# Causal mask of 9 of 12 self tiles by ScalarE, three score buffers in the self pass, and two more cross tiles bounded by VectorE

## The chip, the cores and the metric

One NeuronCore of a Trainium2 chip runs the whole kernel. The metric is device time in microseconds (us), the median of a few executions. The engines are PE (TensorE), ACT (ScalarE), DVE (VectorE), POOL (GpSimd) and SP (SyncE, which here only issues DMAs).

## What is computed

One pre-norm decoder layer on x of shape [32, 256, 256] (batch, sequence, width) in fp32, with 16 heads of 16:

```
x = x + selfattn(layernorm(x))          # latent q and kv projections, rotary, 4 kv heads, causal
x = x + crossattn(layernorm(x), ctx)    # q from x, k and v from ctx [32, 256, 256], one mask [256, 256]
x = x + ffn(layernorm(x))               # 256 -> 1024 -> 256, relu, values rounded to an 8-bit float
```

Softmax is exact: the row maximum of each head is subtracted before the exponential, and scores have fp32 accuracy, reached by cutting q and k into three bf16 parts whose six products are stacked along the contraction dimension (96 rows).

## The kernel before, in words

The batch is cut into 16 groups of two sequences (512 tokens, four blocks of 128). `body(i, prev, nxt)` is the software-pipelined loop body: it holds the attention of group i, the end of the cross attention and the feed-forward part of group i-1, and the projections for the self attention of group i+1. Each engine has its own copy of `body`, its instructions in a fixed, hand-written order; semaphores join them. `body(0)` and `body(15)` stand outside the hardware loop, and after `body(15)` comes an END part. One pass of the loop takes about 102.4 us.

Each attention has two passes. In the first, PE computes score tiles of [128 queries, 1024], DVE takes the row maxima of each (`row_max`), and the negated maxima are cut into three bf16 parts (`cut_first`, `cut_second` on ACT, `cut_rest`, `cut_third` on POOL), transposed by PE (`turn_max`), copied by ACT (`maxima`) and put by a small DMA of SP (`put_neg`) below the rows of Q. There is one such chain for each of the two sequences. In the second pass PE computes the transposed scores with the maxima already subtracted (`self_shifted`, `cross_shifted`), ACT takes the exponential into P (`exponentials`), masked places are set to zero or bounded, and PE multiplies with V three tiles later (`times_v`).

On PE the body runs these stages in order:

- E2, second pass of cross attention of group i-1: `attend(1, ...)`, 16 tiles. At t = 1 it holds the first half of the cross keys' projection of group i (`key2(st, 0)`), at t = 3 the transposes for the second sequence's maxima; tiles 8 to 15 wait for that sequence's `put_neg(1, 1)`. At its end stand self tiles 0 and 1 of group i.
- S1, first pass of self attention of group i: 12 tiles (8 with 256 keys of 4 heads, 4 with 128 keys of 8 heads), with the other projections of ctx between them (`tokens "v2"`, `key2(st, 1)`), then `tokens "out2"`.
- E1, second pass of self attention: 12 tiles and 3 steps.
- a middle part with the normalisations' transposes and the projections of group i+1.
- S2, first pass of cross attention of group i: 16 tiles, with the feed-forward products of group i-1 between them.

Score tiles of S1 alternate between two PSUM buffers, `score[0]` and `score[1]`; those of S2 use `o_pair` as a third. In S1 the causal mask of each tile is added by PE itself, with two matmuls of the identity and `causal_q` (lines 1346 and 1356). In S2, 14 of 16 tiles are handled otherwise: ACT writes the mask into the PSUM buffer ahead (`premask`, line 828), and PE's score matmuls accumulate on it. In E2, 12 of 16 tiles have their P bounded by DVE (`bound`, line 1053, an elementwise minimum with `cross_bound`), and tiles 3, 7, 11 and 15 get a mask from PE (line 1424).

SP issues in a fixed order, each DMA after its own wait. In the part around the border of two bodies it is: `put_part("q1", 0)` (three DMAs of 256 KB), `put_neg(1, 0)`, `put_part("k1", 0)`, `put_part("q1", 1)`, `put_part("k1", 1)`, and in the next body `put_neg(1, 1)`, `put_part("q1", 2)`, `put_part("k1", 2)`, the load of x.

Of the kernel before, what the change touches and what calls it, by code (L numbers as in the profile page):

```python
# [20 lines left out]
BATCH, SEQ, DM = 32, 256, 256  # L21
# [20 lines left out]
PROLOGUE = ["xnT1_0", "xnT1_1", "qa", "q0", "q1", "k", "v_0", "v_1", "maskT", "boundT", "bias"]  # L42


def body_users(prev, nxt):
# [8 lines left out]
    attention = (["k2_0"] + p("m2T_1") + ["v2_0", "k2_1", "m1T_0", "v2_1"] + p("out2_0", "out2_1")  # L54
# [71 lines left out]
def layer(nc, d):  # L126
# [9 lines left out]
    with ExitStack() as stack:  # L136
# [33 lines left out]
        causal_q = sb("causal_q", [128, 128], bf16)  # L170
# [68 lines left out]
        cross_bufs = [score[0], score[1], o_pair]  # L239
# [53 lines left out]
        TILE0 = {"S1": 0, "E1": N1, "E2": 2 * N1 + 2 * CROSS_USES[0]}  # L293
        TILES = 2 * N1 + 2 * CROSS_USES[0] + N2
# [8 lines left out]
        BOUNDED = (N1 - 2, 3 * UNITS)  # L303

        def bounded(a, t):


            u, s = t // TPU[a], t % TPU[a]
            if a == 0:
                return t - (t > 2) if t not in (2, N1 - 1) else None  # L310
            return 3 * u + s if s < 3 else None
# [6 lines left out]
        def cross_use(g, t):  # L318

            n = CROSS_BUF[t]  # L320
            return n, g * CROSS_USES[n] + CROSS_BUF[:t].count(n)

        def cross_tile(g, t):

            n, use = cross_use(g, t)
            return (n, use) if n == 2 else (n, g * (TILES // 2) + N1 + CROSS_BUF[:t].count(n))

        def cross_masked(g, t):

            n = CROSS_BUF[t]  # L330
            told = [u for u in range(N2) if u not in PE_MASKED and CROSS_BUF[u] == n]
            return n, g * len(told) + told.index(t)
# [20 lines left out]
        def _(sp):  # L353
# [80 lines left out]
            def body(i, prev, nxt):  # L434
# [23 lines left out]
                if nxt:  # L458
                    sp.wait_ge(small_full[st.bank("v2_1")], st.this("v2_1"))
                    sp.dma_start(ctxT[:, :, :], ctx_v[i + 1]).then_inc(ctx_loaded, 16)  # L460
                    put_part("q1", 0, i + 1)
                put_neg(st, 1, 0)
                if nxt:
                    put_part("k1", 0, i + 1)
# [16 lines left out]
        def _(pool):  # L481
# [14 lines left out]
            G.affine_select(out=causal_q[:, :], in_=causal_q[:, :], compare_op=ALU.is_ge, fill=-BIG,  # L496
# [124 lines left out]
            def body(i, prev, nxt):  # L621
# [3 lines left out]
                if nxt:  # L625
                    inverse_root(0, i + 1)
# [6 lines left out]
                cut_third(0, i, 1)  # L633
                for t in range(N1):
# [8 lines left out]
                if nxt:  # L643
                    rope_products("q1", cosq, sinq, q1s, i + 1)
                    rope_sum("q1", q1s, i + 1)
                    rope_products("k1", cosk, sink, k1s, i + 1)
                    rope_sum("k1", k1s, i + 1)
                    part("q1", 0, whole, part1, i + 1)
                cut_rest(1, i, 0)
                cut_third(1, i, 0)  # L650
                if nxt:
                    rest("q1", i + 1)
# [8 lines left out]
                if prev:  # L661
                    if nxt:
                        n, before = tile("S1", i + 1, 0)
# [15 lines left out]
        def _(act):  # L679
# [52 lines left out]
            def cut_first(a, g, b):  # L732

                last = N1 // GB * (b + 1) - 1
                for t in (last, last - 1) if a == 0 else last_cross_tiles(b):
                    n, before = tile("S1", g, t) if a == 0 else cross_tile(g, t)
# [24 lines left out]
            def exponentials(st, a, g, with_keys=False, last=False):  # L761
# [13 lines left out]
                for t in range(n):  # L775
# [7 lines left out]
                    if t == 1 and with_keys:  # L783
                        keys(st, 0)
# [37 lines left out]

            def premask(g, t):
# [4 lines left out]
                A.activation(cross_bufs[n][:, :, :].rearrange("p c (j k) -> p (c j) k", j=2),  # L828
# [59 lines left out]
            def body(i, prev, nxt):  # L888
                st = BODY(i)
                if prev:  # L890
                    cut_first(1, i - 1, 1)
                    exponentials(st, 1, i - 1, with_keys=True)
                else:
                    keys(st, 0)
# [946 lines left out]
```

## Time and profile before

| | |
|---|---|
| median of 3 executions | 1729.31 us (1727.02 to 1732.74) |
| profiled execution | 1726.77 us, its span 1725.1 us |
| mean granted TensorE clock | 0.982 of full |
| PE matmuls busy | 1617.5 us, 94% of the span |
| DVE, ACT, POOL busy | 67%, 65%, 44% |
| one pass of the loop | 102.4 us |

The span runs from the first to the last instruction of the profiled execution; its own time is 1.7 us more. A busy share is an average over all stages. In a timeline a row gives the start, the time to the end of the last instruction of the row, engine, line, what is written and read, how many instructions, and in brackets how long the engine sat idle before it and what released it.

### The profile page before, as it was taken

What the parts mean: (1) busy time and instruction counts of PE and PEld (TensorE: products, weight loads), DVE (VectorE), ACT (ScalarE), POOL (GpSimd) and SP (SyncE); (2) the same over time, 40 slices, a digit from 0 to 9 for tenths busy, and PEclk for the clock granted to TensorE, in tenths of its full rate; (3) what the DMA queues carried; (4) which work ended last, traced back from release to release, by engine and by line L of the source; (5) the groups of instructions that cost most, each with busy time, mean ns of one, the idle gap of its engine ahead of it and who ended that gap; (6) DMA issues with size and microseconds to landing.
All of it is one profiled execution on the core that took longest, in us unless ns stands there. A gap on an engine that the chain in (4) does not pass through costs nothing.

```text
span 1725.1 us, 33722 instructions
## 1 busy us (share of the span) xinstructions
PE 1617.5 (94%) x11950; PEld 973.6 (56%) x11950; DVE 1159.0 (67%) x1736; ACT 1116.1 (65%) x1733; POOL 753.5 (44%) x1010
## 2 busy tenths in 40 slices
PE   3879999999999999999999999999999999999988
PEld 2445556656555565655656555665655556565555
DVE  4557576685857758586676858668585775857573
ACT  4455675766668566665856567576666856666574
POOL 2252344644345553444545334464434555344410
PEclk7979999999999999999999999999999999999999
DMA  7473453754547374553845546375454737454420
GB/s 182 59 99 70 68 85 65 103 95 64 96 60 107 68 96 90 75 84 57 119 72 81 94 66 89 65 103 95 64 96 60 106 68 96 90 75 73 62 40 13
DMA packets 106238, 140.17 MB, mean 81 GB/s; under 512 B 12385, under 2 KB 74242, under 8 KB 105954
## 3 DMA queue, kind: packets, MB, share of 16 engines
q1 hardware_dynamic: 103090, 130.96, 51.0%
q0 software_dynamic: 2352, 8.26, 1.5%
q10 hardware_dynamic: 768, 0.57, 0.1%
q8 instruction: 18, 0.29, 0.1%
q14 instruction: 10, 0.08, 0.0%
HBM read 21.29 MB, written 8.39 MB: 17 GB/s over the span
## 4 chain that ended last, share of the span: by engine, by line
PE 75%; DMA 9%; ACT 6%; DVE 4%; issue 3%; POOL 2%; SPq 1%; DVEq 0%; ACTq 0%; POOLq 0%
PE o_pair L1457 14%; PE score L1418 8%; PE small L1543 7%; DMA Q<-negT 5%; PE small L1577 5%; PE o_pair L1288 5%; PE small L1288 4%; PE score L1395 3%; PE small L1304 3%; PE score L1341 3%; DVE negmax L1021 2%; PE score L1376 2%; PE small L1470 2%; DMA sums<-o_sb 2%; PE score L1400 2%
## 5 line engine op out<-in xcount | busy, mean ns | idle before, releaser
L1021 DVE TENSOR_REDUCE negmax<-score 128x4 f32<-128x1024 f32 (+1 forms) x384 | 456.9, 1216 | 73.4 <-PE score L1376 47.0
L780 ACT ACTIVATE P<-score 128x1024 f32<-128x1024 f32 x448 | 446.4, 1026 | 74.6 <-PE score L1418 26.4
L1053 DVE TENSOR_TENSOR P<-P,cross_bound 128x1024 f32<-128x1024 f32 x192 | 230.8, 1250 | 88.6 <-ACT P L780 88.5
L1457 PE MATMUL o_pair<-P,V 128*32 128x256 f32 (+1 forms) x4096 | 280.0, 362 | 2.6 <-DVE P L1053 2.4
L828 ACT ACTIVATE score<-cross_q 128x1024 f32<-128x1024 bf16 x192 | 196.3, 1023 | 46.4 <-DVE negmax L1021 42.9
L1418 PE MATMUL score<-Q,K 99*128 99x256 bf16 x1024 | 152.3, 276 | 25.9 <-DMA Q<-negT 24.8
L1457 PEld LDWEIGHTS o_pair<-P,V 128*32 128x32 f32 x4096 | 87.8, 108 | 134.6 <-issue 73.4
L1577 PE MATMUL small<-xnT,w 128*128 128x256 f32 x600 | 157.6, 381 | 0.0
L1418 PEld LDWEIGHTS score<-Q,K 99*128 99x128 bf16 x1024 | 83.7, 98 | 125.7 <-ACT P L780 61.7
L558 POOL TENSOR_TENSOR x<-x,ffn 128x1024 f32<-128x1024 f32 x15 | 32.8, 2189 | 268.9 <-DVE negmax L1021 268.9
L1376 PE MATMUL score<-K,Q 96*128 96x256 bf16 x768 | 121.0, 282 | 9.9 <-ACT score L828 5.4
L508 POOL TENSOR_TENSOR rstd<-vareps,minus_half 128x2 f32<-128x2 f32 x32 | 22.3, 698 | 236.1 <-DVE vareps L1002 236.1
L607 POOL TENSOR_SCALAR_AFFINE_SELECT P<-P 128x512 f32<-128x512 f32 (+1 forms) x160 | 121.7, 761 | 0.0
L1577 PEld LDWEIGHTS small<-xnT,w 128*128 128x128 f32 x600 | 103.4, 190 | 13.7 <-issue 0.2
L773 ACT ACTIVATE o_sb<-o_pair 128x512 f32<-128x512 f32 x128 | 75.9, 593 | 40.9 <-PE o_pair L1457 40.9
L1376 PEld LDWEIGHTS score<-K,Q 96*128 96x128 bf16 x768 | 74.3, 100 | 48.7 <-issue 13.6
L1041 DVE RECIPROCAL rsum<-small 128x16 f32<-128x16 f32 x63 | 16.2, 257 | 119.1 <-PE small L1470 119.1
L1341 PE MATMUL score<-K,Q 96*128 96x256 bf16 x512 | 79.1, 277 | 16.0 <-DVE negmax L1021 8.9
L1021 DVE TENSOR_REDUCE negmax<-o_pair 128x4 f32<-128x1024 f32 x64 | 78.4, 1225 | 18.0 <-PE o_pair L1381 18.0
L1288 PE MATMUL o_pair<-xnT,w 128*128 128x512 f32 x172 | 90.0, 618 | 0.0
L1341 PEld LDWEIGHTS score<-K,Q 96*128 96x128 bf16 x512 | 43.3, 98 | 68.4 <-DVE negmax L1021 36.3
L1086 DVE SCALAR_TENSOR_TENSOR q2f<-small,bq,q2p 128x256 f32<-128x256 f32 x64 | 28.0, 480 | 75.5 <-ACT q2p L813 75.5
(202 smaller groups left out, 3049.4 us busy)
## 6 DMA issues: line engine op xcount, KB each, us to landing
K<-k2p SPq DMA_DIRECT2D x96, 256.0 KB, 6.2
Q<-q2p SPq DMA_DIRECT2D x192, 128.0 KB, 5.2
Q<-q1p SPq DMA_DIRECT2D x90, 256.0 KB, 6.7
x_in<-in_x SPq DMA_DIRECT2D x16, 512.0 KB, 5.3
ctxT<-in_ctx SPq DMA_DIRECT2D x16, 512.0 KB, 7.1
k2f<-q1f SPq DMA_DIRECT2D x32, 256.0 KB, 6.3
inT<-o_sb SPq DMA_DIRECT2D x60, 128.0 KB
o<-inverse SPq DMA_DIRECT2D x60, 128.0 KB
```

What stands on the lines that cost most here:

```text
L607: G.affine_select(out=p, in_=p, compare_op=ALU.is_ge, fill=0.0, base=0, pattern=[[0, heads], [1, 128]], channel_multiplier=-1).then_inc(pr ...
L780: A.activation(P[:, t % 4, :], score[b][:, :, :], ACT.Exp, scale=SCALE).then_inc(score_free[b], 1)
L828: A.activation(cross_bufs[n][:, :, :].rearrange("p c (j k) -> p (c j) k", j=2), cross_q[:, t // 4 % 2, :].unsqueeze(1).broadcast_to([128, ...
L1021: V.tensor_reduce(negmax[:, k, h:h + 1024 // w], s.rearrange("p (h w) -> p h w", w=w), AX.X, ALU.max, negate=True).then_inc(score_free[b], 1)
L1053: V.tensor_tensor(p, p, cross_bound[:, t % 2, :].unsqueeze(1).broadcast_to([128, 4, SEQ]), ALU.min).then_inc(probs_masked[1], 1)
L1288: last = T.matmul(bank[0:rows, :], w[:, c, cols], src[:, c, :], start=c == 0, stop=c == NC - 1)
L1341: T.matmul(score[n][:, j // 2, SEQ * (j % 2):SEQ * (j % 2) + SEQ], Q1[0:KROWS, 4 * s + j, SEQ * b + 128:SEQ * b + 256], K1[0:KROWS, s, SEQ ...
L1376: last = T.matmul(cross_bufs[n][:, c, SEQ * j:SEQ * j + SEQ], Q2[0:KROWS, b, h, 128 * (k % 2):128 * (k % 2) + 128], K2[0:KROWS, h, SEQ * b ...
L1418: last = T.matmul(score[n][:, c, SEQ * j:SEQ * j + SEQ], K2[:, h, SEQ * b + 128 * kb:SEQ * b + 128 * kb + 128], Q2[:, b, h, :], start=j == ...
L1457: last = T.matmul(o_ps[ob][32 * j:32 * j + 32, SEQ * gg + q0:SEQ * gg + SEQ], v, p, start=s == 0, stop=end, tile_position=(0, 32 * j), ski ...
L1543: last = T.matmul(bank[:, DM * k:DM * k + DM], src[:, c, at:at + 128], w[:, c, :], start=c == 0, stop=c == NC - 1)
L1577: last = T.matmul(bank[:, half], w1[:, c, 128 * t:128 * t + 128], xnT3[:, c, half], start=p == 0, stop=c == NC - 1, skip_group_check=True)
```

## The change

- Self score tiles take three buffers in turn (`self_tile`: tile t in buffer t mod 3, `o_pair` third).
- Tiles 3 to 11 of S1 are no longer masked by PE: ACT writes the causal mask ahead (`self_premask`), nine times a body, in between its evictions of `v2` and `k2`. `causal_q` becomes 256 wide, with zeros in its first half. Tiles 0 to 2 keep their two matmuls.
- The first half of the cross keys' projection, `key2(st, 0)`, moves from E2 (t = 1) into S1, in two parts. The order there becomes v2, tile 2, v2, 3, k2, 4, k2, 5, k2, 6, k2, 7, v2, 8, v2, transposes, 9, 10, 11.
- E2: only tiles 3 and 15 are masked by PE; tiles 7 and 11 are bounded by DVE, 14 of 16 in all.
- DVE: `keys_rest` goes from the bounds to row maximum 5 of S1, and the statistics of the next x go behind row maximum 11.
- SP: `put_neg(1, 0)` goes ahead of `put_part("q1", 0)`. ACT and POOL cut the maxima of S2's first sequence somewhat earlier (`cut_first` before `premask` 10, `maxima` at tile 12 and not 13; on POOL the cuts before `rope_sum("k1")`).
- POOL: `inverse_root(0, i + 1)` goes behind the cuts of the second sequence.
- Prologue: 30 matmuls `warm0` without a use, before the `bias` product.

```diff
-        BOUNDED = (N1 - 2, 3 * UNITS)
+        MASK_ADDED = (3, N2 - 1)
+        BOUNDED = (N1 - 2, N2 - len(MASK_ADDED))
...
+        def self_tile(g, t):
+            n = t % 3
+            return n, g * (TILES // 2 if n < 2 else SELF_USES + CROSS_USES[2]) + t // 3
...
+                put_neg(st, 1, 0)
+                if nxt:
                     put_part("q1", 0, i + 1)
-                put_neg(st, 1, 0)
-                if nxt:
                     put_part("k1", 0, i + 1)
...
+            def self_premask(g, t):
+                n, before = self_tile(g, t)
+                act.wait_ge(score_free[n], before)
+                if t % 6 < 4:
+                    A.activation(bufs[n][:, :, :].rearrange("p c (j k) -> p (c j) k", j=2),
+                                 causal_q[:, :].unsqueeze(1).broadcast_to([128, 4, SEQ]),
+                                 ACT.Copy).then_inc(masked[n], 1)
...
-                    exponentials(st, 1, i - 1, with_keys=True)
-                else:
-                    keys(st, 0)
+                    exponentials(st, 1, i - 1)
+                self_premask(i, 3)
+                self_premask(i, 4)
                 values2(st, 0)
-                cut_first(0, i, 0)
-                cut_second(0, i, 0)
+                self_premask(i, 5)
+                keys(st, 0)
+                self_premask(i, 6)
                 keys(st, 1)
                 keys_full(st, 1)
+                self_premask(i, 7)
+                cut_first(0, i, 0)
+                self_premask(i, 8)
+                cut_second(0, i, 0)
+                self_premask(i, 9)
+                values2(st, 1)
+                self_premask(i, 10)
+                maxima(st, 0, 0)
+                self_premask(i, 11)
                 keys_second(st, i, 0)
-                maxima(st, 0, 0)
-                values2(st, 1)
                 keys_second(st, i, 1)
...
-                    if t == 1 and at_end == "scores":
-                        pe.wait_ge(ctx_loaded, 16 * (g + 2))
-                        key2(st, 0)
...
+            def warm(st, name, n):
+                bk = st.bank(name)
+                pe.wait_ge(small_free[bk], st.before(name))
+                for k in range(n):
+                    last = T.matmul(small[bk][:, :], identb[:, :], again(identb, 4), start=True, stop=True)
...
+            warm(PRO, "warm0", 30)
             bk = PRO.bank("bias")
...
-                self_scores(i, [2])
                 if not prev:
                     pe.wait_ge(loaded, 16 * LOADS)
-                    pe.wait_ge(ctx_loaded, 16 * (i + 1))
-                    key2(st, 0)
+                pe.wait_ge(ctx_loaded, 16 * (i + 1))
+                tokens(st, "v2", ctxT, wv2, 0, 0)
+                self_scores(i, [2])
+                tokens(st, "v2", ctxT, wv2, 0, 1)
                 self_scores(i, [3])
-                tokens(st, "v2", ctxT, wv2, 0, 0)
+                key2(st, 0, 0)
                 self_scores(i, [4])
-                tokens(st, "v2", ctxT, wv2, 0, 1)
+                key2(st, 0, 1)
                 self_scores(i, [5])
                 key2(st, 1, 0)
...
                 self_scores(i, [6])
                 key2(st, 1, 1)
                 self_scores(i, [7])
+                tokens(st, "v2", ctxT, wv2, 1, 0)
+                self_scores(i, [8])
+                tokens(st, "v2", ctxT, wv2, 1, 1)
                 turn_max(st, 0, i, 0)
-                self_scores(i, [8])
-                tokens(st, "v2", ctxT, wv2, 1, 0)
                 self_scores(i, [9])
-                tokens(st, "v2", ctxT, wv2, 1, 1)
```

## Rows read from the trace of the kernel before

**Rows 1.** The page, part 1: busy time of each engine.

```profile
PE 1617.5 (94%) x11950; PEld 973.6 (56%) x11950; DVE 1159.0 (67%) x1736; ACT 1116.1 (65%) x1733; POOL 753.5 (44%) x1010
```

**Rows 2.** Timeline of PE, stage E2 of one pass: start, us, instructions.

```profile
849.83 1.04 PE L1418 MATMUL score<-Q,K 99*128 99x256 bf16 x8 [1.62 <-DMA Q<-negT]
850.71 1.88 PE L1288 MATMUL small<-ctxT,wk 128*128 128x512 f32 x4
852.43 1.04 PE L1418 MATMUL score<-Q,K 99*128 99x256 bf16 x8
...
853.95 0.64 PE L1457 MATMUL o_pair<-P,V 128*32 128x256 f32 x8
...
855.63 0.61 PE L1418 MATMUL score<-Q,K 99*128 99x256 bf16 x4
...
857.85 0.61 PE L1418 MATMUL score<-Q,K 99*128 99x256 bf16 x4
...
859.40 0.61 PE L1418 MATMUL score<-Q,K 99*128 99x256 bf16 x4
```

**Rows 3.** The chain that ended last, in order of time: start, us, what.

```profile
843.59 6.11 DMA Q<-negT
...
873.68 2.19 DMA sums<-o_sb
```

**Rows 4.** Timeline of ACT, end of stage S2.

```profile
843.20 0.37 ACT L753 ACTIVATE negT<-small 48x256 bf16<-48x256 bf16 x1
...
848.80 0.23 ACT L739 ACTIVATE negparts<-negmax 128x32 bf16<-128x32 f32 x1
```

**Rows 5.** Timeline of DVE, three bounds of stage E2.

```profile
856.33 3.50 DVE L1053 TENSOR_TENSOR P<-P,cross_bound 128x1024 f32<-128x1024 f32 x3 [0.18 <-ACT P L780]
```

**Rows 6.** Timeline of SP: when DMAs are issued.

```profile
839.71 1.85 SPq L365 DMA_DIRECT2D Q<-q1p  x3
...
855.42 0.76 SPq L407 DMA_DIRECT2D Q<-negT  x1
```

**Rows 7.** One stretch: busy us of each engine, clock, DMA share, GB/s.

```profile
841.00:855.50 14.50, 12.35 (x97) 7.88 (x96) 9.89 (x10) 10.84 (x18) 10.38 (x13) 1.00 0.99 114
```

**Rows 8.** The page, part 5: a premask of ACT.

```profile
L828 ACT ACTIVATE score<-cross_q 128x1024 f32<-128x1024 bf16 x192 | 196.3, 1023 | 46.4 <-DVE negmax L1021 42.9
```

**Rows 9.** Timeline of PE, stage S1 of the same pass.

```profile
872.26 0.61 PE L1341 MATMUL score<-K,Q 96*128 96x256 bf16 x4
...
873.16 0.61 PE L1341 MATMUL score<-K,Q 96*128 96x256 bf16 x4
...
873.83 1.03 PE L1543 MATMUL small<-wv,ctxT 128*128 128x256 f32 x4
874.69 0.61 PE L1352 MATMUL score<-K,Q 96*128 96x128 bf16 x8
875.14 0.60 PE L1356 MATMUL score<-causal_q,identb 128*128 128x512 bf16 x2
...
886.22 1.89 PE L1543 MATMUL small<-wo,inT 128*128 128x256 f32 x8
```

**Rows 10.** Timeline of ACT, stage S1 of the same pass.

```profile
872.39 0.60 ACT L773 ACTIVATE o_sb<-o_pair 128x512 f32<-128x512 f32 x1 [2.10 <-PE o_pair L1457]
...
881.23 0.68 ACT L704 ACTIVATE k2f<-small,bk 128x512 f32<-128x512 f32 x1
881.80 0.63 ACT L722 ACTIVATE k2p<-k2f 128x512 bf16<-128x512 f32 x1
...
884.65 0.64 ACT L711 ACTIVATE V<-small 128x512 f32<-128x512 f32 x1 [1.97 <-PE small L1543]
885.17 0.61 ACT L722 ACTIVATE k2p<-k2f 128x512 bf16<-128x512 f32 x1
```

**Rows 11.** Timeline of PE: the bias product of the prologue, and the first E2.

```profile
32.92 2.07 PE L1629 MATMUL small<-wo,bv 128*128 128x256 f32 x4 [8.92 <-DVE cross_k L1152]
...
126.64 1.89 PE L1418 MATMUL score<-Q,K 99*128 99x256 bf16 x8 [3.26 <-DMA Q<-negT]
```

More of the change, by code:

```diff
@@ L39 @@
 SCALE = HD ** -0.5
-PROLOGUE = ["xnT1_0", "xnT1_1", "qa", "q0", "q1", "k", "v_0", "v_1", "maskT", "boundT", "bias"]
+PROLOGUE = ["xnT1_0", "xnT1_1", "qa", "q0", "q1", "k", "v_0", "v_1", "maskT", "boundT", "warm0", "bias"]
 def body_users(prev, nxt):
@@ L302, in layer @@
         EVICT_AFTER = (4, 6, 8, 11, 12)
-        BOUNDED = (N1 - 2, 3 * UNITS)
+        MASK_ADDED = (3, N2 - 1)
+        BOUNDED = (N1 - 2, N2 - len(MASK_ADDED))
         def bounded(a, t):
[L308 to L311, printed above, removed]
+            added = (2, N1 - 1) if a == 0 else MASK_ADDED
+            return t - sum(m < t for m in added) if t not in added else None
         def tile(phase, g, t):
@@ L316, in tile, with cross_tile, masked_told, masked_use @@
             return n % 2, g * (TILES // 2) + n // 2
-        def cross_use(g, t):
+        def self_tile(g, t):
+            n = t % 3
+            return n, g * (TILES // 2 if n < 2 else SELF_USES + CROSS_USES[2]) + t // 3
+        def cross_tile(g, t):
             n = CROSS_BUF[t]
[L321 to L332, printed above, removed]
+            use = CROSS_BUF[:t].count(n)
+            return (n, g * (SELF_USES + CROSS_USES[2]) + SELF_USES + use) if n == 2 else \
+                (n, g * (TILES // 2) + SELF_USES + N1 // 2 + use)
+        def masked_told(n):
+            return ([("S1", t) for t in range(SELF_PE_MASKED, N1) if t % 3 == n]
+                    + [("S2", t) for t in range(N2) if t not in PE_MASKED and CROSS_BUF[t] == n])
+        def masked_use(phase, g, t):
+            n = t % 3 if phase == "S1" else CROSS_BUF[t]
+            told = masked_told(n)
+            return n, g * len(told) + told.index((phase, t))
         def last_cross_tiles(b):
@@ L662, in body @@
                     if nxt:
-                        n, before = tile("S1", i + 1, 0)
+                        n, before = self_tile(i + 1, 0)
                         pool.wait_ge(score_free[n], before + 1)
@@ L734, in cut_first @@
                 last = N1 // GB * (b + 1) - 1
-                for t in (last, last - 1) if a == 0 else last_cross_tiles(b):
-                    n, before = tile("S1", g, t) if a == 0 else cross_tile(g, t)
+                for t in (last, last - 1, last - 2) if a == 0 else last_cross_tiles(b):
+                    n, before = self_tile(g, t) if a == 0 else cross_tile(g, t)
                     act.wait_ge(score_free[n], before + 1)
@@ L1011, in row_max @@
             def row_max(a, g, t):
-                b, before = tile("S1", g, t) if a == 0 else cross_tile(g, t)
+                b, before = self_tile(g, t) if a == 0 else cross_tile(g, t)
                 dve.wait_ge(score_full[b], before + 1)
-                s = (score[b] if a == 0 else cross_bufs[b])[:, :, :].rearrange("p c n -> p (c n)")
+                s = bufs[b][:, :, :].rearrange("p c n -> p (c n)")
                 if a == 0 and t % 6 >= 4:
@@ L1169, in cross_bounds @@
                         bound(g, t)
-                    if t == 3 and i is not None:
-                        keys_rest(st, i, 0)
                     if t in (9, 13) and i is None:
                         normalise(st, 1, t // 5 - 1, g)
-                    if t == 11 and nxt:
-                        dve.wait_ge(x_loaded, 16 * (i + 2))
-                        block_stats(0, x_in, range(3))
-                if nxt:
-                    norm_stats(0, x_in, i + 1, range(3, NBLK))
             def body(i, prev, nxt):
@@ L1335, in self_scores @@
                     b, s = t // 6, t % 6
-                    n, before = tile("S1", g, t)
-                    if positive(before):
+                    n, before = self_tile(g, t)
+                    by_pe = t < SELF_PE_MASKED
+                    if not by_pe:
+                        _, use = masked_use("S1", g, t)
+                        pe.wait_ge(masked[n], use + 1)
+                    elif n == 2:
+                        for ob in range(2):
+                            if positive(g * UNITS):
+                                pe.wait_ge(o_free[ob], g * UNITS)
+                    elif positive(before):
                         pe.wait_ge(score_free[n], before)
```

90 lines of the change are left out of this document (48 added, 42 removed).

## The prediction, made before the changed kernel ran

> **What bounds the kernel now.** I read the page first: PE's matmuls are busy 94% of the span, the other engines 67% or less [rows 1]. So a pass of the loop is PE's list of work plus PE's waits, and each edit is priced by what it does to PE's list and to PE's waits. Then I read PE's timeline over one pass (848 to 950 us), where two things stand out. First, E2 opens with a wait of 1.62 us for the DMA of the negated maxima [rows 2]. Second, the key projection that follows, 1.72 us from 850.71 to 852.43, fills time in which tile 2 could not have run for long anyway: it needs the buffer of exponential 0. The chain shows why the DMA is late: it takes 6.11 us, while a small transfer issued into an empty queue takes 2.19 [rows 3]. Behind that lies SP's timeline: three 256 KB transfers of q1 are issued at 839.71, ahead of it [rows 6], and from 841 to 855.5 the DMA engines are full, share 0.99 at 114 GB/s [rows 7].
>
> **Part 1, the start of E2: a gain of 1.9 us a pass.** `put_neg(1, 0)` no longer stands behind the q1 transfers, and ACT copies the maxima one premask (1.0 us) sooner, so it is issued at 843.59 - 1.0 = 842.6 and lands about 2.2 later, near 845 [rows 3, 4]. PE is free at 849.83 - 1.62 = 848.2 [rows 2]. Next late is ACT: its cut of the last maxima starts at 848.80 [rows 4], and with the overlap of 0.1 seen between ACT's instructions exponential 0 starts at 848.95 and ends at 849.97 (an exponential has the size of a premask, 1.02 us [rows 8]). Tile 2 then starts at 850.0, tile 3 after exponential 1 at 851.05, scores and mask take 0.44 each, the transposes 0.1, and the first product with V comes at 852.05 instead of 853.95 [rows 2]: 1.9. The key projection's removal is inside this; alone it would give about 0.5, because exponentials pace the start. If the cut by POOL comes late here, exponential 1 waits up to 1.0.
>
> **Part 2, two masks less in E2: 0.44 each.** Two tiles without a mask take 857.85 - 855.63 = 2.22, so 1.11 each, one with a mask 859.40 - 857.85 = 1.55 [rows 2]. Tiles 7 and 11 give 0.88. The cover is DVE's pitch: three bounds take 3.50 with the last about 1.25, so one each 1.13 [rows 5], against 1.11 of PE. Eleven in a row lag 0.2 behind, and the product comes three tiles later. I price it at nothing; should the pitch be 1.25, it costs 0.5.
>
> **Part 3, the second `put_neg`: a new wait of 2.1.** E2's tile 8 needs `put_neg(1, 1)`. Before, that was issued at 855.42, just as the queue ran empty, and tile 8 started at 859.40 without a wait [rows 2, 6]. Now it is issued 1.9 earlier, at 853.5, but the q1 and k1 transfers, issued from 839.71 before, start only behind the first `put_neg`, at 842.6 + 0.8 = 843.4, 3.7 later. They move the same bytes at full DMA share [rows 7], so they end near 855.2 + 3.7 = 858.9, and the small transfer, behind them in the same queue, lands near 859.2. Tile 8 is due at 859.40 - 1.9 - 0.44 = 857.06. PE waits 2.1. Nothing else of PE's list can pass it: the products with V stand behind. Bounds: 0, if the small transfer slips through in 2.2 us, and 3.9 more than a free one, the excess of the 6.11 over the 2.19 [rows 3], which gives up to 3.9. I take 2.1, nearer to what the first one shows. The Trainium skill says the same of the queue (DMA: Bandwidth & Descriptors, Queues, rings and completion order): on each DMA engine the descriptors of one issuing queue are consumed in ring order. By that rule the transfer cannot land before the backlog in front of it, and it speaks against moving q1 behind; the 6.11 us agrees.
> E2 in all: -1.9 - 0.88 + 2.1 = -0.7.
>
> **Part 4, S1: 2.7 us longer.** Before, from the last product of E2 to `out2` PE needs 886.22 - 872.26 = 13.96 [rows 9]. After, its own work is: v2 and k2 in eight pieces of 0.87 (874.69 - 873.83; a piece of k2 has as many columns), 6.9; tile 2 with mask 873.83 - 873.16 = 0.67; nine tiles of 0.44 to 0.45 (875.14 - 874.69), 4.0; transposes 0.1. That is 11.7. If ScalarE kept ahead, S1 would gain 2.3. But ACT's list interleaves premasks with evictions that must wait for PE, and PE's next tile waits for the premask behind the eviction. From the end of issue of a projection piece it is 0.19 until ACT starts (row 873.83 lasts 1.03 against 0.87 to the next, and a releaser adds 0.03), a key eviction takes 0.57 (881.80 - 881.23), an eviction of v2 0.52 (885.17 - 884.65) [rows 10], a premask 1.02, and 0.06 until PE starts.
> - Tile 6 waits for premask 6, behind `keys(0)`: 0.19 + 0.57 + 1.02 + 0.06 = 1.84, of which tile 5 and a k2 piece cover 1.31. Wait 0.5.
> - Tile 7 stands directly behind the last k2 piece, and its premask behind `keys(1)` and `keys_full(1)`: 0.19 + 2 x 0.57 + 1.02 + 0.06 = 2.4, nothing covers it. Wait 2.4.
> - Tile 10, behind `values2(1)`: 0.19 + 0.52 + 1.02 + 0.06 = 1.8, less transposes and tile 9, 0.56. Wait 1.2.
> - Tile 11: `maxima` (0.37 less overlap, about 0.3) and a premask (pitch 0.94) after tile 10, less 0.44. Wait 0.8.
> Sum 4.9 to 5.0, so S1 takes 16.7 instead of 13.96: +2.7. ACT starts on its premasks on time, right behind the eviction at 872.39. DVE is not the bound: twelve maxima of about 1.2, one reciprocal and `keys_rest` fit in between. The first chain of maxima lands before E1 (its DMA finds a free queue: 2.2 after `maxima`, which is 1.7 before E1 starts with `out2` in between), and the statistics now behind row maximum 11 end 0.4 before PE needs the bank that DVE's next instruction frees. So E1 follows without a new wait, and middle and S2 keep their length.
> The bounds of this term: 2.0, if the handovers between engines are each 0.1 to 0.2 shorter, and 3.5, if `out2`'s chain or E1's first DMA slips too.
>
> **Part 5, the ends.** The first E2 waits 3.26 for the DMA [rows 11]; at a low clock its projection is dear too. I take -3.5 there, and no wait at tile 8, as its tiles are slow. `warm0`: the bias product runs at half clock, 2.07 us for four matmuls that take 1.03 later [rows 9, 11]. Thirty matmuls of 512 columns at 0.43, falling to 0.22, take about 9 us from 32.92, in a gap that ends at about 41: bias, and behind it DVE's last rotary steps, are 2 to 3 us later, but group 0's S1 runs at full clock. +0.5, S1 of group 0 included. END has two masks less: -0.9.
>
> **The sum.** Fourteen passes of -0.7 + 2.7 = +2.0 give +28; the first pass -3.5 + 2.7 = -0.8; prologue +0.5; END -0.9. In all +27. The profiled execution took 1726.8 us, so 1754; the median of the three runs lies 2.5 above it, so 1757.
>
> **Rivals.**
> - The transfer is in time (0.18). The 24 KB slip through the backlog and tile 8 doesn't wait; then E2 gains 2.8, S1 loses 2.7, they nearly cancel, and with part 5 the time is about 1727. For it: rings are many, and the small rows may find a free one. Against: the 6.11 us.
> - Faster (0.14). The place is tiles 6, 7, 10 and 11 of S1. If their waits sum to 2.5 and not 5, S1 costs 0.2, a pass gains 0.5, and the time with part 5 is about 1719; with no waits at all 1681. It decides once the sum falls under 3.0. For it: PE removes 2.9 us of mask matmuls. Against: the order of ACT's list.
> - The clock falls (0.10). S1 becomes thin for PE (11.7 busy of 16.7). If the granted clock drops to its lower level of 1.2 GHz after tile 7's gap, the remaining 5.3 us of S1 and `out2` take twice as long, less the 2 us of waits that this hides: 3 more a pass, about 1800. Against: the wait of 1.62 before E2 left the clock at 1.00 in the stretch around it [rows 7]. The Trainium skill (TensorE: Matmul & The Clock Gate, HAM oscillation) describes loops that go back to half rate at each gap. No row here shows a gap of 2.4 us in a full pass.
> - Slower otherwise (0.08): POOL's cut is late in E2, or DVE's pitch is 1.25; 1765 to 1775.
> - My forecast has 0.50, with a range of its own of 1740 to 1774.
>
> **How the numbers follow.** 0.3% (5 us) is about what a measurement of this kernel can tell from no change. Slower: 0.50 + 0.10 + 0.08 and a little of the first rival, 0.72. Same: 0.12. Faster: 0.14 and a part of the first rival, as first pass and END gain, 0.16. The range goes from 1722, which leaves out the lower half of the faster case, to 1778, which leaves out the clock's.
>
> **What would show it.** In the profile after: no wait of line 1418 at E2's tile 0; a wait of 1 to 4 us for DMA Q<-negT at its tile 8; in S1 waits of PE for ACT's premask of about 0.5, 2.4, 1.2 and 0.8; S1 near 16.7; a pass near 104.4. ACT busy about 150 us more (16 x 9 x 1.02), PE about 55 us less. The prediction is wrong if ACT's premasks run ahead of PE in S1, if tile 8 doesn't wait, or if the clock falls.

## The result, and the profile of the changed kernel

The changed kernel takes 1874.24 us (median of 4 executions, 1872.49 to 1875.28) against 1728.94 for the kernel before (4 executions): 1.084 times the time, with an interval of 1.0823 to 1.0856. That is 145 us more, far above the forecast range. The page of the changed kernel, its part 1 and the clock line of part 2:

```profile
PE 1664.0 (89%) x11628; PEld 978.2 (52%) x11628; DVE 1201.6 (64%) x1768; ACT 1257.0 (67%) x1877; POOL 753.3 (40%) x1010
...
PEclk9979989999899998999999899998999999899999
```

PE has 322 matmuls fewer than in [rows 1], and yet it is busy 46.5 us longer. So the instructions are slower on average, and the mean granted clock fits that: 0.937, where it was 0.982. PE's waits, by what ended them (us in all, how many, the longest in us):

```profile
PE score L1446 <- DMA Q<-negT: 54.3, 14, 3.9
...
PE score L1372 <- ACT score L837: 43.0, 33, 2.3
```

The first comes once in a pass, at tile 8 of E2. The second comes twice, at tiles 6 and 7 of S1, hence the 33. Now one pass, stage E2, on PE's timeline (answers to [rows 2]):

```profile
913.04 1.04 PE L1619 MATMUL small<-w2q,hq 128*128 128x256 fp8e4 x8
913.91 1.22 PE L1446 MATMUL score<-Q,K 99*128 99x256 bf16 x8
915.93 0.61 PE L1446 MATMUL score<-Q,K 99*128 99x256 bf16 x4 [0.80 <-ACT P L791]
...
918.05 0.64 PE L1486 MATMUL o_pair<-P,V 128*32 128x256 f32 x8
...
927.08 1.03 PE L1446 MATMUL score<-Q,K 99*128 99x256 bf16 x4 [3.94 <-DMA Q<-negT]
928.04 1.08 PE L1486 MATMUL o_pair<-P,V 128*32 128x256 f32 x8
...
933.69 0.64 PE L1486 MATMUL o_pair<-P,V 128*32 128x256 f32 x8
```

Tile 0 has no wait any more, tile 8 waits 3.94. And look at the second number of each row: the same eight products take 0.64 at 918.05, 1.08 at 928.04 and 0.64 again at 933.69. The chain and SP's timeline show what tile 8 waits for (answers to [rows 3, 6]):

```profile
919.43 7.53 DMA Q<-negT
```

```profile
908.51 0.79 SPq L417 DMA_DIRECT2D Q<-negT  x1
909.42 1.88 SPq L375 DMA_DIRECT2D Q<-q1p  x3
...
914.55 1.25 SPq L373 DMA_DIRECT2D K<-k1p  x2
919.43 0.76 SPq L417 DMA_DIRECT2D Q<-negT  x1
920.45 0.57 SPq L375 DMA_DIRECT2D Q<-q1p  x1
921.07 0.58 SPq L373 DMA_DIRECT2D K<-k1p  x1
```

Stage S1 on PE's and on ACT's timeline (answers to [rows 9, 10]):

```profile
942.24 1.13 PE L1569 MATMUL small<-wv,ctxT 128*128 128x256 f32 x4
...
947.84 1.08 PE L1311 MATMUL small<-ctxT,wk 128*128 128x512 f32 x2
949.25 0.61 PE L1372 MATMUL score<-K,Q 96*128 96x256 bf16 x4 [0.34 <-ACT score L837]
949.70 1.02 PE L1311 MATMUL small<-ctxT,wk 128*128 128x512 f32 x2
953.00 0.61 PE L1372 MATMUL score<-K,Q 96*128 96x256 bf16 x4 [2.27 <-ACT score L837]
953.45 1.56 PE L1569 MATMUL small<-wv,ctxT 128*128 128x256 f32 x4
...
955.65 1.81 PE L1569 MATMUL small<-wv,ctxT 128*128 128x256 f32 x4
957.29 0.28 PE L1582 MATMUL small<-identb,negparts 128*128 128x128 bf16 x2
957.40 0.60 PE L1372 MATMUL score<-K,Q 96*128 96x256 bf16 x4
959.09 0.62 PE L1379 MATMUL score<-K,Q 96*128 96x128 bf16 x8 [1.08 <-ACT score L841]
960.29 0.76 PE L1379 MATMUL o_pair<-K,Q 96*128 96x128 bf16 x8 [0.58 <-ACT o_pair L841]
960.84 3.53 PE L1569 MATMUL small<-wo,inT 128*128 128x256 f32 x8
964.21 1.03 PE L1423 MATMUL score<-Q,K 99*128 99x512 bf16 x4
```

```profile
950.76 0.69 ACT L709 ACTIVATE k2p<-small,bk 128x512 bf16<-128x512 f32 x1 [1.56 <-PE small L1311]
951.35 0.68 ACT L715 ACTIVATE k2f<-small,bk 128x512 f32<-128x512 f32 x1
951.92 1.03 ACT L837 ACTIVATE score<-causal_q 128x1024 f32<-128x1024 bf16 x1
```

ACT's three rows are tile 7's wait: it stands idle until the last piece of k2 is there, evicts it twice, and only then writes the mask that PE has been waiting for since 950.7. The windows over these stages, with columns as in [rows 7]:

```profile
913.00:925.00 12.00, 8.91 (x86) 4.44 (x84) 9.37 (x8) 9.52 (x13) 3.81 (x6) 1.00 1.09 118
925.00:933.00 8.00, 5.92 (x36) 1.91 (x36) 2.49 (x3) 2.86 (x3) 0.00 (x0) 0.59 0.68 107
933.00:941.00 8.00, 8.00 (x85) 3.75 (x82) 6.93 (x6) 6.08 (x8) 0.00 (x0) 0.98 0.05 17
941.00:952.00 11.00, 9.39 (x65) 5.26 (x63) 9.31 (x9) 6.85 (x10) 2.99 (x2) 1.00 0.31 94
...
955.00:957.00 2.00, 2.00 (x9) 1.60 (x7) 1.11 (x1) 0.07 (x1) 2.00 (x3) 0.50 0.00 0
957.00:960.00 3.00, 1.63 (x16) 0.94 (x14) 1.59 (x3) 2.51 (x4) 3.00 (x4) 0.96 0.00 0
...
962.00:964.00 2.00, 2.00 (x7) 1.55 (x6) 1.96 (x10) 0.46 (x2) 0.49 (x2) 0.50 1.02 152
964.00:966.00 2.00, 2.00 (x11) 1.38 (x10) 1.65 (x5) 1.07 (x2) 1.03 (x1) 0.99 1.10 119
```

The clock falls to its lower level, 1.2 GHz, three times in a pass. Behind tile 8's wait it stays there for some 6 us, until 933. Behind tile 7's wait it is low from about 954 to 957. From there to 960 it is back at 2.4 GHz: tile 9's scores, at 957.40, take the 0.60 of full speed. Then, behind the waits of 1.08 and 0.58 at tiles 10 and 11, it falls once more and is back at 964, which makes `out2` slow. From 925 to 933, 5.92 us of PE's work hold 36 instructions; from 933 to 941, 8.00 us hold 85.

A pass takes 112.7 us, 10.3 more than before. By stage, from the starts of the rows above, of [rows 2, 9], and of the last feed-forward products before:

```profile
847.17 1.04 PE L1593 MATMUL small<-w2q,hq 128*128 128x256 fp8e4 x8
```

| stretch | before | after | change |
|---|---|---|---|
| last feed-forward product to first product with V | 6.78 | 5.01 | -1.8 |
| on to tile 8 of E2 | 5.45 | 9.03 | +3.6 |
| tile 8 to the end of E2 | 12.86 | 15.16 | +2.3 |
| S1 | 13.96 | 18.60 | +4.6 |
| out2 | 1.72 | 3.37 | +1.6 |

They add up to 10.3 or so, which leaves next to nothing for the other stages. Fourteen to fifteen such passes make the 145.

### The profile page after: what moved, and what is told of

It reads as the page before. It is cut to its first block, busy times and chain, and to the rows that moved or that the text cites. A ratio compares the mean times of both kernels' runs of the same rounds, so it can differ in the third digit from the quotient of the medians.

```text
span 1873.0 us, 33411 instructions
## 1 busy us (share of the span) xinstructions
PE 1664.0 (89%) x11628; PEld 978.2 (52%) x11628; DVE 1201.6 (64%) x1768; ACT 1257.0 (67%) x1877; POOL 753.3 (40%) x1010
## 4 chain that ended last, share of the span: by engine, by line
PE 74%; ACT 9%; DMA 7%; issue 5%; DVE 4%; POOL 1%; ACTq 0%; SPq 0%; DVEq 0%; POOLq 0%
PE o_pair L1486 11%; PE small L1569 10%; DMA Q<-negT 6%; PE score L1446 5%; PE small L1603 5%; PE o_pair L1311 4%; PE small L1311 4%; PE score L1404 3%; PE small L1619 3%; PE score L1423 3%; PE small L1327 3%; PE score L1372 2%; ACT P L791 2%; PE small L1499 2%; ACT score L837 2%
## 5 line engine op out<-in xcount | busy, mean ns | idle before, releaser
L1051 DVE TENSOR_REDUCE negmax<-score 128x4 f32<-128x1024 f32 x320 | 386.5, 1217 | 98.9 <-PE score L1404 43.3
L1083 DVE TENSOR_TENSOR P<-P,cross_bound 128x1024 f32<-128x1024 f32 x224 | 269.4, 1246 | 129.6 <-ACT P L791 129.5
L1486 PE MATMUL o_pair<-P,V 128*32 128x256 f32 (+1 forms) x4096 | 300.2, 384 | 3.4 <-DVE P L1083 3.2
L1446 PE MATMUL score<-Q,K 99*128 99x256 bf16 x1024 | 178.1, 303 | 74.9 <-DMA Q<-negT 54.3
L1051 DVE TENSOR_REDUCE negmax<-o_pair 128x4 f32<-128x1024 f32 (+1 forms) x128 | 156.3, 1221 | 56.3 <-PE o_pair L1384 22.4
L1404 PE MATMUL score<-K,Q 96*128 96x256 bf16 x768 | 119.7, 280 | 13.1 <-ACT score L850 8.8
L525 POOL TENSOR_TENSOR negrest<-negmax,negparts 128x32 f32<-128x32 f32 x64 | 16.5, 258 | 235.7 <-ACT negparts L750 235.7
L1404 PEld LDWEIGHTS score<-K,Q 96*128 96x128 bf16 x768 | 73.7, 99 | 51.4 <-ACT score L850 14.6
L1372 PE MATMUL score<-K,Q 96*128 96x256 bf16 x384 | 58.3, 274 | 43.0 <-ACT score L837 43.0
L1569 PE MATMUL small<-wv,ctxT 128*128 128x256 f32 x256 | 86.9, 474 | 0.0
```

Of the source, the lines that this page charges most:

```text
L1051: V.tensor_reduce(negmax[:, k, h:h + 1024 // w], s.rearrange("p (h w) -> p h w", w=w), AX.X, ALU.max, negate=True).then_inc(score_free[b], 1)
L1083: V.tensor_tensor(p, p, cross_bound[:, t % 2, :].unsqueeze(1).broadcast_to([128, 4, SEQ]), ALU.min).then_inc(probs_masked[1], 1)
L1372: last = T.matmul(bufs[n][:, j // 2, SEQ * (j % 2):SEQ * (j % 2) + SEQ], Q1[0:KROWS, 4 * s + j, SEQ * b + 128:SEQ * b + 256], K1[0:KROWS, ...
L1404: last = T.matmul(bufs[n][:, c, SEQ * j:SEQ * j + SEQ], Q2[0:KROWS, b, h, 128 * (k % 2):128 * (k % 2) + 128], K2[0:KROWS, h, SEQ * b:SEQ * ...
L1446: last = T.matmul(score[n][:, c, SEQ * j:SEQ * j + SEQ], K2[:, h, SEQ * b + 128 * kb:SEQ * b + 128 * kb + 128], Q2[:, b, h, :], start=j == ...
L1486: last = T.matmul(o_ps[ob][32 * j:32 * j + 32, SEQ * gg + q0:SEQ * gg + SEQ], v, p, start=s == 0, stop=end, tile_position=(0, 32 * j), ski ...
```

## The experiments

Two theories stand against each other: the waits alone (for the DMA and for the masks) cost the time, or the waits together with the clock that falls behind them.

**One edit taken back: the order of the first small transfer.** `e1_q1_first` is the changed kernel with

```diff
+                if nxt:
+                    put_part("q1", 0, i + 1)
                 put_neg(st, 1, 0)
                 if nxt:
-                    put_part("q1", 0, i + 1)
                     put_part("k1", 0, i + 1)
```

> The changed kernel, with the first q1 transfers issued ahead of put_neg(1, 0) again. Queue theory (the q1 and k1 transfers, moved behind the first small transfer, delay the second one): the wait of 3.94 us at tile 8 of E2 and the low clock after it (2.7 us) go, a wait of 0.5 to 1.0 at tile 0 comes back; a pass shrinks from 112.7 by about 6, to 106.6, and the time falls from 1874 to about 1789. S1 stays at 18.6 us. Rival (the low clock has another cause, such as the thin S1): the wait goes, but the clock stays low in E2; 1874 - 15 x 3.2 = 1826. Rival (the second small transfer is slow by itself): nothing changes.

Measured 1825.51 us, ratio 1.0558 (1.0533 to 1.0582), a pass 109.2. Tile 8 waits no more. Tile 0 does, for longer than before the change, and the low clock comes in the rows behind it, after two more waits of 0.76 and 0.42:

```profile
894.96 1.04 PE L1447 MATMUL score<-Q,K 99*128 99x256 bf16 x8 [2.42 <-DMA Q<-negT]
...
897.79 1.03 PE L1447 MATMUL score<-Q,K 99*128 99x256 bf16 x4 [0.42 <-ACT P L792]
```

So the edit alone is worth 49 us of the 145. The number is by chance that of the first rival, 1826, but the rival had the clock low in E2 without a wait; in the trace the rows behind tile 8 run at full speed. The expected time was too low for three reasons. Tile 0's wait is 2.42 and not 0.5 to 1: the q1 transfers are issued at 884.87, 6.6 us ahead of the last feed-forward product, where it was 7.5 before the change, and in both kernels the small transfer lands 10.0 us behind that issue. The low clock follows this wait too. And there is a new wait of 1.08 in E1, for the small DMA of S1's maxima. In the changed kernel, where `out2` is slow, it does not show; here `out2` runs at full clock in every pass, though the four waits of S1 are the same.

**One edit alone: the same order in the kernel before.** `e5_before_swap`:

```diff
                     sp.dma_start(ctxT[:, :, :], ctx_v[i + 1]).then_inc(ctx_loaded, 16)
+                put_neg(st, 1, 0)
+                if nxt:
                     put_part("q1", 0, i + 1)
-                put_neg(st, 1, 0)
-                if nxt:
                     put_part("k1", 0, i + 1)
```

> The kernel before, with one edit: put_neg(1, 0) ahead of put_part(q1, 0) on SP, as the change has it. Queue theory: the wait of 1.62 us at E2's tile 0 goes and one of 2 to 4 us comes at tile 8, with the low clock after it (2.7 us); a pass gets 3 to 5 us longer and the time is 1775 to 1805. Rival (the late second transfer comes from something else in the change, such as the shorter E2 start): E2 shrinks by 1.6 and the time is about 1705.

Measured 1795.23 us, ratio 1.0379 (1.0359 to 1.0400), as expected. Moving one small DMA ahead of three large ones costs 66 us, with the low clock behind the new wait as part of it:

```profile
889.83 0.61 PE L1418 MATMUL score<-Q,K 99*128 99x256 bf16 x4 [2.88 <-DMA Q<-negT]
```

**The order of ACT in S1.** `e2_premask_first` is the changed kernel with each premask ahead of the eviction that made it late:

```diff
                 self_premask(i, 5)
+                self_premask(i, 6)
                 keys(st, 0)
-                self_premask(i, 6)
+                self_premask(i, 7)
                 keys(st, 1)
                 keys_full(st, 1)
-                self_premask(i, 7)
...
+                self_premask(i, 10)
                 values2(st, 1)
-                self_premask(i, 10)
+                self_premask(i, 11)
                 maxima(st, 0, 0)
-                self_premask(i, 11)
```

> The changed kernel, with ACT's premasks of S1 ahead of the evictions that wait for PE (premask 6 before keys(0), 7 before keys(1), 8 behind keys_full, 10 before values2(1), 11 before maxima). Order theory (PE's waits in S1 come from ACT's order, and the low clock after them from the waits): the waits of 2.3 and 1.1 us go, the clock stays at 1.00 through S1, S1 takes 14 to 15 us and not 18.6, out2 1.7 and not 3.4; a pass shrinks by about 6 and the time is about 1784. Rival (ACT's total work of nine premasks is what makes S1 long, in whatever order): S1 stays near 18 us and the time above 1850. E2's wait of 3.9 stays in both.

Measured 1821.93 us, ratio 1.0537 (1.0511 to 1.0562). S1 takes 928.95 - 914.60 = 14.35 instead of 18.60, and `out2` behind it runs at full clock. But E2's wait of 3.84 stays, and E1 now waits twice:

```profile
928.49 0.62 PE L1379 MATMUL o_pair<-K,Q 96*128 96x128 bf16 x8 [0.84 <-ACT o_pair L841]
928.95 1.95 PE L1569 MATMUL small<-wo,inT 128*128 128x256 f32 x8
931.75 1.03 PE L1423 MATMUL score<-Q,K 99*128 99x512 bf16 x4 [0.86 <-DMA Q<-negT]
...
940.28 0.60 PE L1423 MATMUL score<-Q,K 99*128 99x512 bf16 x2 [1.30 <-DMA Q<-negT]
```

It is 38 us slower than expected, and these two, 2.2 us a pass, are most of that: the small DMAs of S1's maxima are late next.

**The clock by itself.** `e3_fill` leaves both waits as long as they are. It puts matmuls that nobody reads into them, 18 before tile 8 of E2 and 7 before tile 7 of S1:

```diff
+            def dummy(bk, before, n):
+                pe.wait_ge(small_free[bk], before)
+                for k in range(n):
+                    T.matmul(small[bk][:, :], identb[:, :], again(identb, 4), start=True, stop=True)
...
+                    if t == n // 2 and at_end == "scores":
+                        dummy(st.bank("v2_0"), st.before("v2_0"), 18)
...
                 key2(st, 1, 1)
+                dummy(st.bank("v2_1"), st.before("v2_1"), 7)
                 self_scores(i, [7])
```

> The changed kernel with matmuls without a use in its two largest waits: 18 of 512 columns into a free bank before E2's tile 8 waits for its DMA, 7 before S1's tile 7 (PE's order only; nothing else moves). It measures the clock's part alone. Clock theory: the waits stay for the other engines, but the granted clock stays at 1.00, and the 2.7 us of E2 and the 3.5 us of S1 and out2 that run at 1.2 GHz go: 1874 - 15 x 6.2 = about 1781. Rival (the waits alone cost what was lost, and the clock's part is small): above 1850.

Measured 1816.72 us, ratio 1.0507 (1.0482 to 1.0531), mean clock 0.981. PE's rows around tile 8:

```profile
898.10 4.06 PE L1293 MATMUL small<-identb 128*128 128x512 bf16 x18
902.02 0.61 PE L1452 MATMUL score<-Q,K 99*128 99x256 bf16 x4
```

Work without a use made the kernel 57 us faster: the wait is as long as before, but the tile behind it takes 0.61 and not 1.03. The waits of the changed kernel alone would thus have given 1817 or less, and the clock did the rest. Or less, because the clock is not held everywhere: behind S1's last two waits, 1.09 and 0.57, `out2`'s first eight matmuls take 1.95 in nine of fifteen passes, and 3.0 to 3.6 in the other six. The time lies 36 us above the expected one and 33 below the rival's. The wait of 1.08 in E1 comes out here in the passes where `out2` is fast, some 10 us in all, and the six slow rows make some 8; the other 18 were not looked into.

**Both edits of order.** `e4_both` is the first and the third experiment together.

> Both edits, q1 transfers first and premasks first. If the two causes add up: 1874 - 85 - 90 = about 1700, faster than before (1729) by 1.7%, as two masks less in E2 and S1 at 14.2 us remain. If the rest of the change has a cost of its own (DVE's longer list, the projection moved into S1), it ends at 1729 or above.

Measured 1786.26 us, ratio 1.0332 (1.0308 to 1.0357): 86 us too high. At tile 0 of E2 the wait is back, with a second one of 0.76 behind it and then rows at low clock; two more, 0.86 and 1.24, are in E1:

```profile
871.99 1.04 PE L1447 MATMUL score<-Q,K 99*128 99x256 bf16 x8 [2.45 <-DMA Q<-negT]
873.79 2.07 PE L1447 MATMUL score<-Q,K 99*128 99x256 bf16 x8 [0.76 <-ACT P L792]
```

Here my expectation fell, that the edits would take 85 and 90 us away. Alone they took 49 and 52, together 88. The kernel needs an order in which neither small transfer is issued while many large ones are still under way.

**Such an order.** In `e6_split`, again the changed kernel, the second part of q1 and k1 moves behind the second small transfer:

```diff
                     put_neg(st, 1, 1)
+                    put_part("q1", 1, i)
+                    put_part("k1", 1, i)
                     put_part("q1", 2, i)
...
                     put_part("k1", 0, i + 1)
-                    put_part("q1", 1, i + 1)
-                    put_part("k1", 1, i + 1)
```

> The changed kernel, with put_part(q1, 1) and put_part(k1, 1) moved behind put_neg(1, 1), so that each of the two small transfers has at most one batch of large ones in front of it. Queue theory: no wait at tile 0 of E2, none at tile 8, clock 1.00 in E2; S1 as in the changed kernel (18.4 to 18.6 us); a wait of about 1.1 at tile 6 of E1 appears as in e1. Against e1_q1_first (1825.5) a pass gains the difference of the waits at tile 0, 2.4 against none, so about 1800. Rival (the bytes of both batches delay whatever comes after): the wait moves to self tile 0, which needs all of q1 and k1, and the time stays at 1825 or above.

Measured 1778.00 us, ratio 1.0280 (1.0259 to 1.0300), a pass 105.9. No wait for a DMA is left in E2; S1's four waits are unchanged. The place of the four DMAs that moved had thus made 96 of the 145 us, the low clock in E2 included. The time is 22 us below the expected one: the wait that was expected in E1 comes only in the two passes of fifteen in which `out2` runs at full clock, and in the first.

**The clock in S1 by itself.** `e10_split_fill` is `e6_split` with `e3_fill`'s second edit, the 7 unused matmuls before tile 7 of S1.

> e6_split with seven matmuls without a use in the wait before S1's tile 7: the low clock's price in S1 and out2 alone. Clock theory: S1's other waits stay, the granted clock stays at 1.00 and about 3.5 us of S1 and out2 go, of which E1 may give back 1.1 in its wait at tile 6: 1778 - 15 x 2.5 = about 1741. Rival (the clock falls because S1 as a whole is thin, whatever is done in its one large gap): 1770 or more.

Measured 1753.34 us, ratio 1.0135 (1.0101 to 1.0170): 25 us less than `e6_split`, and nearer to the clock theory's 1741 than to its rival's 1770. S1 takes 794.78 - 777.95 = 16.83, where the forecast had 16.7. The row behind it still shows the low clock, as it does in six of fifteen passes:

```profile
777.95 1.13 PE L1575 MATMUL small<-wv,ctxT 128*128 128x256 f32 x4
...
794.78 3.61 PE L1575 MATMUL small<-wo,inT 128*128 128x256 f32 x8
```

**All of it in order.** `e7_best` has `e6_split`'s SP, `e2_premask_first`'s ACT, and

```diff
-                self_premask(i, 11)
                 maxima(st, 0, 0)
+                self_premask(i, 11)
...
                 put_neg(st, 0, 0)
-                put_part("k2", 0, i)
                 put_neg(st, 0, 1)
-                for n in range(1, 3):
+                for n in range(3):
```

> The split order of e6, the premasks ahead of the evictions as in e2, and for E1: maxima ahead of premask 11 on ACT, both small transfers of S1 ahead of all k2 transfers on SP. If every lost microsecond has been named (waits at tiles 0 and 8 of E2, S1's order, waits of 0.9 and 1.2 in E1, the clock after them): a pass takes 101.2 us, against 106.2 in e4_both, and the time is about 1712, faster than before by 1%. If the change's other parts cost something, 1729 or more. If the DMAs only move their delay, 1750 or more.

Measured 1702.34 us, ratio 0.9842 (0.9826 to 0.9859), clock 0.981, a pass 100.7: the first version that beats the kernel before, by 1.6%, and 10 us better than expected. S1 takes 771.36 - 756.78 = 14.58, with three small waits, the last of them

```profile
770.91 0.62 PE L1378 MATMUL o_pair<-K,Q 96*128 96x128 bf16 x8 [1.08 <-ACT o_pair L840]
```

**Two masks back on PE.** `e11_best_masks` is `e7_best` with `MASK_ADDED = (3, 7, 11, N2 - 1)`, as before the change.

> e7_best with E2's tiles 7 and 11 masked by PE again, as before the change. If each of them costs PE 0.44 and DVE has room for it: 16 x 0.88 = 14 us more than e7_best (1702), 1716. Rival (DVE's pitch or the exponentials bound E2 then, so PE's masks are hidden): 1702 to 1706.

Measured 1715.61 us, ratio 0.9922 (0.9895 to 0.9950): 13.3 us over 16 passes is 0.83, where Part 2 said 0.88.

**Without the warming matmuls.** `e8_no_warm` is the changed kernel without `warm0`.

> The changed kernel without the 30 matmuls of warm0 in the prologue. By my prediction they cost up to 0.5 us in group 0; by the trace after, the first E1 starts 3.4 us later than before, of which the late bias product is about 2.3. So the time is 1872, 2 us less than with them. Rival (they save time by the clock that they raise): 1877.

Measured 1878.53 us, ratio 1.0860 (1.0842 to 1.0878). The expected time was 1872, the rival's 1877. The interval overlaps that of the changed kernel, so the time doesn't decide. In the trace the first S1 is slow at its start, and E1 begins at 66.94, where it begins at 65.46 with them. The expected gain of 2 us didn't come.

**The split order in the kernel before.** `e9_before_split` is `e5_before_swap` with the split of `e6_split`.

> The kernel before, with SP's order alone changed: put_neg(1, 0) first, then one batch of q1 and k1, put_neg(1, 1), then the other batch. Queue theory: the wait of 1.62 at tile 0 goes and none comes at tile 8; about 1.5 a pass, twice that in the first, so about 1705. Then nearly all that e7_best (1702) gains over the kernel before is SP's order, and the premasks of S1 give nothing. Rival (e7_best's gain comes from PE's shorter list): 1725 or more.

Measured 1781.27 us, ratio 1.0294 (1.0267 to 1.0322), where I expected a gain, to 1705. There DVE takes the statistics of the next x in the midst of the bounds, and x is loaded behind all the parts that moved. DVE's row, then PE's:

```profile
895.91 1.08 DVE L990 BATCH_NORM_STATS2 stats<-x_in 128x6 f32<-128x256 f32 x3 [3.73 <-DMA x_in<-in_x]
```

```profile
898.17 1.08 PE L1457 MATMUL o_pair<-P,V 128*32 128x256 f32 x8 [2.30 <-DVE P L1053]
```

The low clock follows this wait as well. The changed kernel takes these statistics behind row maximum 11; there the split brings no such wait.

**Everything but S1.** `e12_no_s1` is the kernel before with the split order, the statistics behind row maximum 11, the earlier cuts on ACT and POOL, and 14 bounded tiles. It has no premask in S1, `key2(st, 0)` is still in E2, and there is no `warm0`:

```diff
+        MASK_ADDED = (3, N2 - 1)
+        BOUNDED = (N1 - 2, N2 - len(MASK_ADDED))
...
-                    if t == 11 and nxt:
-                        dve.wait_ge(x_loaded, 16 * (i + 2))
-                        block_stats(0, x_in, range(3))
-                if nxt:
-                    norm_stats(0, x_in, i + 1, range(3, NBLK))
...
+                if nxt:
+                    dve.wait_ge(x_loaded, 16 * (i + 2))
+                    norm_stats(0, x_in, i + 1)
```

> Everything of the change but its edits of S1 (no premasks of self tiles, two buffers, key2 still in E2) and warm0, with SP's split order: the statistics of x behind row maximum 11, the earlier cuts on ACT and POOL, 14 bounds on DVE. In e9_before_split DVE waited 3.73 us for x_in ahead of its bounds, since x is loaded behind all q1 transfers; here that wait is off the path. By the rows: a start of E2 1.6 earlier and two masks of 0.44 less give 2.5 a pass, so about 1729 - 16 x 2.5 = 1689, faster than e7_best (1702): then S1's new form costs about 0.8 us a pass even in its best order. Rival (S1's new form pays): 1705 to 1720. Rival (DVE, with keys_rest and 14 bounds in E2, is the bound there): 1710 or more, with waits for DVE at line 1053.

Measured 1697.03 us, ratio 0.9808 (0.9794 to 0.9821), a pass 100.4. It lies between the 1689 expected and the 1705 of the rival. It is the fastest of all, and its interval lies below that of `e7_best`. Even in the best order tried here the new S1 doesn't pay: 14.6 us against the 13.96 of [rows 9], and the projection that it took out of E2 makes E2's start only 0.15 shorter there (5.02 in `e7_best`, 5.17 here, from the last feed-forward product to the first product with V). The two kernels differ in `warm0` and in the order around E1 as well, so the 5 us between them are not S1's alone. One wait of S1 is left:

```profile
760.34 0.61 PE L1336 MATMUL score<-K,Q 96*128 96x256 bf16 x4 [0.76 <-DVE negmax L1021]
```

## Why the prediction was wrong

The direction was right, the time was not: 1757 forecast, 1874 measured. The step that failed is the clock: the forecast left it at full speed behind two new waits of over 2 us, and the runs show it low three times a pass, for 6.2 us. Step by step:

- **Part 1** (start of E2, -1.9) held: -1.8, with ACT's exponentials setting the pace (the 0.80 at 915.93).
- **Part 2** (two masks, -0.88 a pass) held: 0.83 in `e11_best_masks`.
- **Part 3** (tile 8, +2.1 of wait) had the right mechanism and the wrong size: 3.94. The issue time was right, 6.4 us behind the last feed-forward product where 6.3 was forecast. The transfer took 7.53 and not 5.7, so it landed 1.8 us later than my subtraction of issue times made it. A part of that is a row that I misread: the 2.19 us are those of an 8 KB transfer, behind one of 128 KB and not in an empty queue [rows 3]. One of the 24 KB transfers that met no backlog took 2.87 (issued at 928.76 in `e2_premask_first`). I had both bounds and took the value by calculation, where the upper one, from the row of 6.11, was the better guide. What part the transfers issued at 920.45 to 922 have in it was not tried. The Trainium skill's sentence on ring order (DMA: Bandwidth & Descriptors, Queues, rings and completion order) pointed the right way: the transfer did not slip past.
- **Part 4** (S1, +2.7 from four waits) held. A row counts a wait from the modelled end of the matmul before, so the price is read from start to start: tile 6 comes 949.25 - 947.84 - 0.87 = 0.54 late, tile 7 953.00 - 949.70 - 0.87 = 2.43, tile 10 959.09 - 957.40 - 0.44 = 1.25, tile 11 960.29 - 959.09 - 0.44 = 0.76. That is 4.98, forecast 4.9 to 5.0. The 11.7 of own work and these make the 16.7 forecast; the measured 18.60 has 1.9 more, nearly all of it in the rows at low clock.
- **"E1 follows without a new wait"** was right only because `out2` was slow. In `e1` to `e4` and `e10`, in the passes where `out2` ran at speed, E1 waited 0.9 to 1.3 once or twice for S1's small DMAs.
- **Part 5**: `warm0` was put at +0.5 with S1 of group 0. The two traces say it gains 1.5; the times leave it open.
- **The step that failed is "the clock falls"**, which stood as a rival and not in the sum, with a chance of 0.10, at 3 us a pass, and tied to tile 7's gap alone. It should have been a consequence of the main forecast: that had itself put two waits of over 2 us into a pass, where [rows 7] only showed the clock holding around 1.62. The trace of the kernel before had a row for it, which I overlooked: at 1643.40 PE waits 2.37, outside the loop, and the four matmuls at 1645.40 take 1.91 where such a row takes 1.03. Measured, the clock fell behind both long waits, and a third time behind the two short ones of tiles 10 and 11. Its price is 2.7 us in E2 (15.16 against the 12.42 that the stretch takes with one mask less), 1.9 in S1, and 1.65 in `out2`, together 6.2 a pass. The runs give a net price of at least 57 us for the two long waits (`e3_fill`) and 25 for S1's (`e10_split_fill`): less than 6.2 a pass, since E1's hidden wait comes out and some passes keep the low clock in `out2`.

Put together: -0.7 + 2.7 was the forecast pass. Part 3 adds 1.9, the clock 6.2, which makes 10.1 against the 10.3 measured. The Trainium skill (TensorE: Matmul & The Clock Gate, HAM oscillation) describes a loop that pays for the clock again at every gap, and I set it aside with one row of a shorter gap. The trace agrees with the loop: each pass shows it, behind 2.27 and 3.94 us, and behind 1.08 and 0.58 close together.

That the two orders are to blame, and not the idea as a whole, is shown by `e7_best`. That the masks by ACT in S1 brought nothing in the orders tried is what `e12_no_s1` points to. Of the gain of that version the two masks are 0.8 us of some 2 a pass; the rest is the order of the DMAs with what makes it possible, and that rest wasn't split further.

## What to carry to other kernels

When a forecast puts a new wait of a few us on TensorE, first ask what the clock does behind it, look in the trace for a wait as long and the rows behind it, and put the stretch that follows at the lower level into the main sum. A wait that cannot be removed can be filled with matmuls. A small DMA on which the critical engine waits must be ordered against the large ones on both sides, those behind it at the first place and those ahead of it at the next. When ScalarE prepares a buffer for TensorE, its preparation must stand ahead of the eviction of the piece that TensorE computes right before, or TensorE waits for its own result to be carried off.

## What the hardware showed that was not expected

- The clock fell behind waits of 3.94, 2.88, 2.30 and 2.27 us. In `e1_q1_first` and `e4_both` it fell behind 2.42 and 2.45, in the passes shown after one or two shorter waits had followed. In the kernel before it held behind the waits at tile 0 of E2, 1.55 to 1.65, in thirteen passes.
- The length of one wait doesn't decide it. S1 has the same waits of 1.08 and 0.58, 1.2 us apart, ahead of `out2` in five runs. `out2` was slow behind them in all fifteen passes of the changed kernel, in thirteen of `e6_split`, in six of `e3_fill` and of `e10_split_fill`, and in none of `e1_q1_first`. What decides between them was not found.
- Once down, the clock stayed low for 6 us of full work in E2 (927 to 933), and for about 3 us each in S1 and `out2` (954 to 957, 961 to 964).
- A DMA of 24 KB took 2.87 us when it met no backlog (`e2_premask_first`), and 7.53 with ten others issued ahead of it. The number of those ahead is not all: behind the same three of 256 KB it took 6.11, issued 3.9 us after the first of them [rows 3, 6], and 7.85 in `e1_q1_first`, issued 2.1 us after. Both landed 10.0 us after the first was issued.
- Matmuls that nobody reads, 18 and 7 of them in two waits that they could not shorten, gave back 57 us, a little more than the 52 of mending ACT's list.
